# A second layernorm fed from centred summands instead of from the first one's finished output

## What is computed

```
t = t + _L0_ffn_ref(_ln_t(t), ...)         # layer 0's experts; their output is out
#   _L0_ffn_ref ends with
#   out = _layer_norm(out + x, gamma, beta)  # (v - mean) * rsqrt(var + 1e-5) * gamma + beta, over channels
x = _from_tokens(t, x)
x = x + _L1_conv_ref(_ln_c(x), ...)        # layer 1's mixer; _ln_c: (v - mean) / sqrt(var + 1e-6), over channels
#   _L1_conv_ref begins with 1x1, 3x3 and 5x5 convolutions of its input, summed
```

## Time and profile before

| what | value |
|---|---|
| median of 3 runs | 191.16 us (191.05 to 191.4) |
| the profiled execution's own time | 190.52 us |
| its span, first to last instruction | 188.7 us |
| granted TensorE clock, mean | 1.0 of full speed |
| busy: TensorE / its weight loads | 176.2 us (93%) / 87.0 us (46%) |
| busy: VectorE / ScalarE / GpSimd | 116.7 (62%) / 123.9 (66%) / 44.8 us (24%) |

### The profile page before, as it was taken

One profiled execution on the slowest core, in us unless ns is written; L12 is line 12 of the kernel. 1 busy time (PEld: TensorE's weight loads), 2 busy tenths in 40 slices (PEclk: granted clock), 3 DMA queues, 4 the chain that ended last, 5 costly groups with the idle time before them and its releaser, 6 DMA issues.

```text
span 188.7 us, 3175 instructions
## 1 busy us (share of the span) xinstructions
PE 176.2 (93%) x1185; PEld 87.0 (46%) x1191; DVE 116.7 (62%) x312; ACT 123.9 (66%) x201; POOL 44.8 (24%) x62
## 2 busy tenths in 40 slices
PE   7999999999997999999999999999999996999991
PEld 2554324449786574322222355452224895353230
DVE  1476889758732744946545353586575798587565
ACT  2465997745438776765765650587775897588772
POOL 6162412000100102005973000020760022030660
PEclk9999999999999999999999999999999999999999
DMA  6999700000000000000000000000000000000001
GB/s 204 401 423 414 280 2 0 0 0 3 5 0 0 3 0 3 0 0 0 0 3 2 0 0 0 0 0 3 0 2 0 3 2 2 3 0 0 0 0 56
DMA packets 3088, 8.56 MB, mean 45 GB/s; under 512 B 521, under 2 KB 1041, under 8 KB 2945
## 3 DMA queue, kind: packets, MB, share of 16 engines
q1 hardware_dynamic: 2736, 7.73, 10.3%
q0 software_dynamic: 192, 0.50, 0.7%
q10 hardware_dynamic: 144, 0.13, 0.3%
HBM read 8.10 MB, written 0.26 MB: 44 GB/s over the span
## 4 chain that ended last, share of the span: by engine, by line
PE 67%; DVE 13%; ACT 8%; POOL 6%; issue 4%; POOLq 1%; ACTq 0%; DVEq 0%
PE bank L454 13%; PE banks L386 7%; PE banks L312 7%; PE banks L387 6%; POOL total L1620 6%; PE bank L325 5%; PE banks L650 4%; PE bank L317 4%; PE banks L369 3%; ACT hidden L893 2%; ACT rstd L861 2%; PE bank L434 1%; PE banks L625 1%; PE bank L397 1%; ACT sq_sim L979 1%
## 5 line engine op out<-in xcount | busy, mean ns | idle before, releaser
L893 ACT ACTIVATE hidden<-banks,pack_l 128x1024 f32<-128x1024 f32 x40 | 44.5, 1112 | 17.3 <-PE banks L387 16.6
L454 PE MATMUL bank<-hidden,w 128*64 128x512 f32 (+1 forms) x144 | 37.1, 593 | 0.7 <-ACT hidden L893 0.7
L386 PE MATMUL banks<-split_x,w_hi 128*128 128x512 f16 x64 | 24.6, 384 | 0.0
L387 PE MATMUL banks<-split_x,w_lo 128*128 128x512 f16 x64 | 24.3, 379 | 0.0
L312 PE MATMUL banks<-idle_work 128*128 128x512 bf16 x66 | 18.4, 408 | 1.5 <-DVE idle_work L1199 1.2
L1620 POOL TENSOR_TENSOR total<-total,term 128x512 f32<-128x512 f32 x12 | 17.1, 1422 | 1.9 <-DVE term L1176 1.3
L1597 POOL CAST split_x<-normed 64x256 f16<-64x256 f32 x12 | 6.1, 505 | 45.8 <-DVE normed L1081 42.1
L386 PEld LDWEIGHTS banks<-split_x,w_hi 128*128 128x128 f16 x64 | 6.2, 97 | 22.4 <-issue 13.4
L857 ACT ACTIVATE squares<-bank 128x256 f32<-128x256 f32 x18 | 6.9, 383 | 14.3 <-PE bank L317 12.8
L454 PEld LDWEIGHTS bank<-hidden,w 128*64 128x64 f32 x144 | 7.2, 134 | 14.1 <-issue 12.5
L1176 DVE TENSOR_TENSOR term<-relu_sim,bank 128x512 f32<-128x512 f32 x12 | 7.8, 684 | 7.8 <-PE bank L397 5.3
(11 more groups left out here) (320 smaller groups left out, 325.3 us busy)
## 6 DMA issues: line engine op xcount, KB each, us to landing
w_stage<-in_w SPq DMA_DIRECT2D x3, 512.0 KB, 12.7
w_stage<-in_w SPq DMA_DIRECT2D x1, 1024.0 KB, 9.2
conv<-in_conv SPq DMA_DIRECT2D x1, 800.0 KB, 7.3
w<-in_w SPq DMA_DIRECT2D x3, 256.0 KB, 12.9
w<-in_w SPq DMA_DIRECT2D x1, 512.0 KB, 9.9
toeplitz<-in_toeplitz SPq DMA_DIRECT2D x1, 512.0 KB, 10.5
gauss<-in_gauss SPq DMA_DIRECT2D x1, 512.0 KB, 12.0
pack_l<-in_pack_l SPq DMA_DIRECT2D x1, 469.0 KB, 11.3
```

The costliest lines, as they stand in the source:

```text
L386: mm(out, w1_hi[l][:, at:at + 128], split_x[h][:, :], start=True, stop=False)
L387: last = mm(out, w1_lo[l][:, at:at + 128], split_x[h][:, :], start=False, stop=True)
L454: last = mm(out[64 * h:64 * h + 64, cut], w2[l][:, (f * NE + e) * CH:(f * NE + e + 1) * CH], hidden[v % 3][:, h * 512 + cut.start:h * 512 ...
L893: act(hidden[u % 3][:, :], both[u % 2][:, :], ACT.Gelu, bias=P(f"l{l}", "e_b1")[:, e * fc + f:e * fc + f + 1]).then_inc(S["moe_gelu"], 1)
```

## The change

C is the centring matrix. Centring x2 gives C·x2 = C·diag(gamma)·C·total times the root, plus C·(x1 + beta), since the root is one number per pixel. The kernel now makes the 128x128 matrix C·diag(gamma)·C on the chip, at its start (VectorE: `gamma_rows`; TensorE: one product into `bank[3]`; ScalarE: a copy into `both_centred`). At the seam TensorE makes `both_centred` times `total` (`centred_scaled`) and C times `x1_beta` (`centred_input`), the latter for chunk 0 ahead of the last expert's `down`. VectorE multiplies the first by norm 2's root and adds the second; the sum is norm 3's centred input, in SBUF. ScalarE squares it from there. Norm 3's root goes into `rnorm`, so that norm 2's stays in `rstd`. x2 itself is made later on VectorE, behind the rounding rests. The filler after layer 0's experts is gone, and those in front of norm 3's averages are one each.

```diff
-        LAYER_TAIL = [1, 5, 6, 0]
+        LAYER_TAIL = [0, 5, 6, 0]
...
+        centred_x1 = (bank[1][:, 0:PIX], bank[3][:, PIX:2 * PIX])
...
+            def centred_input(j):
+
+                pe.wait_ge(S["x1_beta"], 1)
+                mm(centred_x1[j], P("first", "center"), chunk(x1_beta, j), start=True, stop=True)
+
+            def centred_scaled(j):
+
+                mm(bank[2 + j][:, 0:PIX], both_centred[:, :], chunk(total, j), start=True, stop=True)\
+                    .then_inc(S["x2_terms"], 1)
...
+                if l == 0:
+                    centred_input(0)
                 down(units - 1)
...
+            pe.wait_ge(S["gamma_centre"], 1)
+            mm(bank[3][:, 0:128], P("first", "center"), gamma_rows[:, :], start=True, stop=True).then_inc(S["gamma_centre"], 1)
+            busy(NORM_TAIL[0], bank[0][:, :])
             for j in range(INNER):
                 pe.wait_ge(S["l0_xn"], j + 1)
+                if j:
+                    pe.wait_ge(S["gamma_centre"], 3)
...
-            norm(2, total, lambda j: pe.wait_ge(S["l0_term"], 2 * L0_KEPT + j + 1))
-
-
-
-            for j in range(INNER):
-                center(3, j, x[2], x_ready(2))
-                busy(2, bank[0][:, :])
-                average(3, j)
+            for j in range(INNER):
+                center(2, j, total, lambda j: pe.wait_ge(S["l0_term"], 2 * L0_KEPT + j + 1))
+            for j in range(INNER):
+                average(2, j)
+            centred_scaled(0)
+            centred_input(1)
+            centred_scaled(1)
+            busy(1, bank[0][:, :])
+            average(3, 0)
+            busy(1, bank[0][:, :])
+            average(3, 1)
             busy(NORM_TAIL[3], bank[0][:, :])
...
-                act(chunk(squares, j), bank[4 + j][:, 0:PIX], ACT.Square).then_inc(S["ln_squared"], 1)
+                act(chunk(squares, j), chunk(normed[3], j) if k == 3 else bank[4 + j][:, 0:PIX], ACT.Square)\
+                    .then_inc(S["ln_squared"], 1)
...
+            sc.wait_ge(S["gamma_centre"], 2)
+            act(both_centred[:, :], bank[3][:, 0:128], ACT.Copy).then_inc(S["gamma_centre"], 1)
...
+            ve.wait_ge(S["first_loaded"], 16)
+            ve.wait_ge(S["l0_loaded"], 16)
+            TS(gamma_rows[:, :], P("first", "center"), P("l0", "gamma"), None, ALU.mult).then_inc(S["gamma_centre"], 1)
...
-            ve.wait_ge(st.sem, x1b)
-            for j in range(INNER):
-                norm_chunk(2, j)
+            for j in range(INNER):
+                ve.wait_ge(S["ln_rstd"], 2 * 2 + j + 1)
+                ve.wait_ge(S["x2_terms"], j + 1)
+                TT(chunk(term[1], j), bank[2 + j][:, 0:PIX], chunk(rstd, j), ALU.mult).then_inc(S["ln_out"], 1)
                 ve.wait_ge(S["ln_out"], 2 * 2 + j + 1)
-                STT(chunk(x[2], j), chunk(normed[2], j), P("l0", "gamma"), chunk(x1_beta, j), ALU.mult, ALU.add)\
-                    .then_inc(S["x_ready"], 1)
-
-
-            for j in range(INNER):
-                norm_chunk(3, j)
+                TT(chunk(normed[3], j), centred_x1[j], chunk(term[1], j), ALU.add).then_inc(S["ln_centered"], 1)
+
+            for j in range(INNER):
+                ve.wait_ge(S["ln_rstd"], 2 * 3 + j + 1)
+                ve.wait_ge(S["ln_squared"], 2 * 3 + j + 1)
+                TT(chunk(normed[3], j), chunk(normed[3], j), chunk(rnorm, j), ALU.mult).then_inc(S["ln_out"], 1)
                 for h in range(HALVES):
                     ve.wait_ge(S["v_hi"], 2 * j + h + 1)
                     here, other = slice(64 * h, 64 * h + 64), slice(64 - 64 * h, 128 - 64 * h)
                     TT(chunk(padded[h], j)[other, :], chunk(normed[3], j)[here, :], chunk(padded[h], j)[here, :],
                        ALU.subtract).then_inc(S["v_lo"], 1)
+            ve.wait_ge(S["x1_beta"], 1)
+            for j in range(INNER):
+                st.link(TT(chunk(normed[2], j), bank[4 + j][:, 0:PIX], chunk(rstd, j), ALU.mult))
+                STT(chunk(x[2], j), chunk(normed[2], j), P("l0", "gamma"), chunk(x1_beta, j), ALU.mult, ALU.add)\
+                    .then_inc(S["x_ready"], 1)
```

More of the change, by code:

```diff
@@ L127, in metaformer @@
             w1_split0 w1_split1 w1_split2 w1_split3 w2_loaded0 w2_loaded1 w2_loaded2 w2_loaded3 x_loaded
-            x_ready y_ps z_ps z_rows""".split()
+            gamma_centre x1_beta x2_terms x_ready y_ps z_ps z_rows""".split()
         S = {n: sem(n) for n in names}
@@ L217, in metaformer @@
         context = sb("context", [128, 128])
+        gamma_rows = sb("gamma_rows", [128, 128])
+        both_centred = sb("both_centred", [128, 128])
         mix = sb("mix", [128, 128])
@@ L501, in _ @@
             pe.wait_ge(S["first_loaded"], 16)
-            norm(0, x[0], lambda j: pe.wait_ge(S["x_loaded"], 16))
+            for j in range(INNER):
+                center(0, j, x[0], lambda j: pe.wait_ge(S["x_loaded"], 16))
+            for j in range(INNER):
+                average(0, j)
+            pe.wait_ge(S["gamma_centre"], 1)
+            mm(bank[3][:, 0:128], P("first", "center"), gamma_rows[:, :], start=True, stop=True).then_inc(S["gamma_centre"], 1)
+            busy(NORM_TAIL[0], bank[0][:, :])
             for j in range(INNER):
                 pe.wait_ge(S["l0_xn"], j + 1)
+                if j:
+                    pe.wait_ge(S["gamma_centre"], 3)
                 for h in range(HALVES):
@@ L856, in square @@
                 sc.wait_ge(S["ln_centered"], 2 * k + j + 1)
-                act(chunk(squares, j), bank[4 + j][:, 0:PIX], ACT.Square).then_inc(S["ln_squared"], 1)
+                act(chunk(squares, j), chunk(normed[3], j) if k == 3 else bank[4 + j][:, 0:PIX], ACT.Square)\
+                    .then_inc(S["ln_squared"], 1)
             def inverse_deviation(k, j):
                 sc.wait_ge(S["ln_variance"], 2 * k + j + 1)
-                act(chunk(rstd, j), variance_ps(k, j), ACT.Abs_reciprocal_sqrt,
+                act(chunk(rnorm if k == 3 else rstd, j), variance_ps(k, j), ACT.Abs_reciprocal_sqrt,
                     bias=P("first", "eps6" if LN_EPS[k] == 1e-6 else "eps5")).then_inc(S["ln_rstd"], 1)
@@ L1305, in _ @@
             weight = lambda e, j: l0_weight[:, j * 8 + e:j * 8 + e + 1]
-            x1b = st.mark(TS(x1_beta[:, :], x[1][:, :], P("l0", "beta"), None, ALU.add))
+            TS(x1_beta[:, :], x[1][:, :], P("l0", "beta"), None, ALU.add).then_inc(S["x1_beta"], 1)
             for e in range(L0_KEPT):
```

## The result

The changed kernel takes 191.85 us (median of 18 runs) against 191.13 us of the kernel before in as many runs beside it: ratio 1.0037, 95% interval 1.0022 to 1.0053. It is slower by 0.7 us, with an interval of 0.4 to 1.0. The forecast was 191.5 us, range 191.0 to 192.0. The time lies in the range, but the case I thought likeliest was "no change", and the excess over the kernel before is twice the 0.33 us that I had worked out.

The account below looks back on a forecast made before the run. It took the engine-to-engine relay, VectorE's nearly gapless queue (0.13 us slack) and TensorE's channel-gate wait as bounds. Front minus 0.50, queue plus 1.73, less slack and overlap, gave plus 0.33: 191.5 us, range 191.0 to 192.0.

Parts of the forecast that it names:

- no change: Whole kernel: time within about 0.2% (0.38 us) of the kernel before; chance 0.45.
- Edits that I cost at nothing: x1's centring before the last down, 0 to plus 0.1 us; start's matrix product, 0 to plus 0.22; filler removal, nothing or minus 0.1.
- The front: Layernorm relay from layer 0's last expert to the first convolution tap: convolution starts 0.50 us earlier, at 42.48.
- Point 1: At the seam, the both_centred product stands behind two averages, ends at 37.89; VectorE's root product starts 37.92, 0.28 us late.
- Points 2 to 4: Relay after the root product: ScalarE's square starts 0.53 us earlier, SBUF reading adds 0.03, the rest keeps its shapes.
- the prediction's own sign: Front is wrong if the first tap does not move by half a microsecond.
- The queue: x2's four VectorE instructions before the weights' split take 1.73 us; channel gate's second product comes 0.33 us later, at 51.13.
- Sum: Front minus 0.50, queue plus 1.73, slack and earlier convolution used up, overlap regained minus 0.16: net plus 0.33 us.
- Absorbed: Rival: TensorE's stop at the channel gate costs nothing later, the 0.50 us stay won, 190.7 us; chance 0.12.
- Products not late: Rival: at the seam the root ends last, front gains 0.78, total plus 0.05, 191.2 us; chance 0.10.
- Clock: Rival: TensorE's clock falls in the new gap at 49.4, up to 4 us more, 195 us; chance 0.04.
- GpSimd's squaring over the scaling: Rival: before the channel gate, delayed squaring holds VectorE's mean scaling to 50.4, plus 0.25 us, 191.7 us; chance 0.14.

Follow-up runs that it names:

- Experiments 2: Changed kernel with the centring of x1's first chunk moved from ahead of the last expert's down product to behind the first both_centred product; ratio to the kernel before 1.0013.
- experiment 4: Changed kernel with x1's first chunk centred in the same place by two products of 64 output columns each; ratio to the kernel before 1.0014.
- experiment 7: Kernel before plus one centring product of x1's first chunk ahead of the last expert's down product, result unused; ratio 1.0012.
- experiment 8: Changed kernel with x2 in VectorE's gaps, x1's centring later, one start filler less, and first both_centred product between the averages; ratio to the kernel before 0.9985.
- experiment 1: Changed kernel with x2's four instructions moved from ahead of the weights' split into VectorE's gaps; ratio to the kernel before 1.0004.
- experiment 6: Kernel before plus four VectorE instructions of x2's shapes between the rounding rests and neg_scale, each waiting for the last, result unused; ratio 1.0048.
- experiment 9: Changed kernel with x2 in gaps, one start filler less, x1's centring as 64-column halves before the last down, both_centred product between averages; 189.86 us, ratio to before 0.9945.
- experiments 5: Changed kernel with x2 in VectorE's gaps, x1's centring behind the first both_centred product, and four start fillers instead of five; ratio to the kernel before 0.9971.

## Why the prediction was right and where it was wrong

**The step that failed is the paragraph "Edits that I cost at nothing"**, in two of its terms. For x1's centring I put 0 to 0.1 us, because 0.25 us of idle time and 0.27 of overlap made room for a product of 0.43. Experiments 2, 4 and 7 show 0.31 (0.30 in experiment 7): the overlap of load and tail, which I added to the room, is just what is lost when a 128-column product stands between 64-column ones. I had seen that overlap between products of one shape only, and took it for a property of all. The Trainium skill, "TensorEngine Tiling (Array Packing)", section "Key Properties", says that a change of the tiling mode drains the engine. The traces fit that, with 0.31 us for one product there and back and with 64-column passes that run in pairs; the page has no figure. The kernel declares no tiling mode, so that the drain is the mechanism is argued from the two idle stretches of the loads and not shown. For the start I put 0 and had plus 0.22 as a bound; it was plus 0.16: the cover was there for a quarter of the product only.

**The front.** Point 1 had the right wait and nearly its size. The product by the root is 1.67 us behind the averages' start; I had 1.59. TensorE's product ends as worked out (38.34 + 0.59 = 38.93, 1.56 behind 37.37), but VectorE starts 0.11 later and not 0.03. The step in between is a semaphore instruction of VectorE's own: an instruction carries one wait here, and of two waits the other stands ahead of it as an instruction by itself. In the trace that for TensorE's product (line 1360) comes at 38.98, and the product by the root 0.06 behind it. In experiment 8 the sum has the same step (38.98, then 39.05). The kernel before has it too, in its chain of waits between the root's end (37.54) and VectorE's 37.64, and I had not counted it:

```profile
37.57 0.02 DVEq L1080
```

The chain of waits of the changed kernel names another releaser (start us, length us, what):

```profile
38.11 0.92 ACT rstd L889 x2
...
39.04 0.44 DVE term L1361
```

It names ScalarE's roots, because the second chunk's ends at 39.03 by coincidence. The code waits for the first one's, and in experiment 8 VectorE's product starts at 38.19, when the second root (38.55) is not yet begun. Points 2 to 4, from there to the first tap, were 4.56 us forecast and measured. So the front gained 10.34 - 10.23 = 0.11 us from the last but one `down` to the first tap, where 0.50 was forecast: 0.31 went in the slot and 0.08 in the late start. By the prediction's own sign, a first tap that moves by half a microsecond, the front was wrong.

**The queue.** 1.73 us forecast, 1.72 measured. The first product of the gate follows the maximum by 0.56 us (0.60 forecast), the second the first by 0.70 (0.71). One small gain was missing in the sum: the maximum starts 0.08 us before the recorded end of the low part of the weights, where I let 0.03 pass. Behind the gate nothing had slack, as said. Of the 1.72 us only 0.67 come through (experiment 1): 0.19 go at the maximum, 0.69 at the gate's first product, to which TensorE comes 1.25 us behind the maximum when it has not to wait (49.12 and 50.37 in experiment 1) and now 0.56, and 0.17 between the gate's two products, mostly in the shorter `ca_in`.

**Sum.** Forecast plus 0.33. To that come 0.31 (slot), 0.08 (late product) and 0.16 (start), and off it about 0.11 for the maximum and 0.05 for the rest up to the gate: 0.72, where the distances give 0.70. The forecast's distance to the edge of "no change" was 0.05 us, so a mis-sized term of 0.3 was enough to turn the case. That the time still lies in the range is partly luck: the slot went 0.21 us past its bound, and 0.16 us of gains that the sum did not have made up for most of it.

**The rivals.** *Absorbed*: falls by experiments 1 and 6. *Products not late*: falls, they are late by 0.36; with them in time (experiment 9) the front gives 0.85. *Clock*: all forty slices stay at nine. In experiments 5 and 8 the last slice falls to seven, but the clock's record falls there at 186.0 and 186.6 us, behind TensorE's last product (184.0 and 184.2), and the time from the exponentials to the end is as before (133.6). *GpSimd's squaring over the scaling*: half of it happens. In experiment 6 the squaring starts at 51.22 under the low part of the weights and takes 0.96 us in place of 0.61; counted back from its end it ran from 51.57, 0.06 ahead of the maximum that follows VectorE's instruction. In the changed kernel it is 0.71 long for the same reason (51.37 - 0.61 = 50.76, again 0.06 ahead of the maximum). The Trainium skill, "SBUF — State Buffer", section "SBUF: two separate sides", says that such a pair block each other for a whole instruction; both rows agree. But the scaling, with one tensor input of one element per partition, ran in full beside the squaring, 0.14 us at 51.95 (51.15 in the changed kernel), so the 0.25 us of this rival did not come. And `ca_in` was 0.15 long, as forecast.

Not shown: the start's 0.16 in timed runs, where it is smaller than the intervals, and what sets the moment at which the clock's record begins.

## What to carry to other kernels

A gap between TensorE's products takes in another one at the price of its passes only if it has its neighbours' weight width (0.01 against 0.31 us here): read from the record what two neighbours of different shape cost, and not only how long the gap is. When an intermediate result leaves the relay and is still needed later, it has to go into measured idle time; put in front of a chain it costs its length less all the slack behind it, which has to be read at every engine that the chain passes (here 1.72 us became 0.67). A product that is taken off a path helps only if every input of the next instruction is early as well: move one and read which is last now.

## What the runs showed of the hardware that was not expected

- One product of full width between 64-column ones costs 0.30 us more than the same work in two halves, whose passes run in pairs (slot 1.65 and 1.35 us, changed kernel and experiment 4; 1.64 in experiment 7).
- The first eleven products of a program take 3.90 to 4.88 us from one execution to the next, with the same instructions, because their spacing halves (0.43 to 0.22 us) at a moment that lies anywhere from 3.95 to 7.02 us, where the trace's record of the clock begins. A comparison of two single spans of this kernel is uncertain by at least that much.
- On VectorE a chain in which each instruction waits for the one ahead cost 0.98 us for a pair, where a pair with one such wait cost 0.86 (experiment 6).
- A scaling of one element per partition with one tensor input (0.14 us) runs unhindered beside a GpSimd squaring that a long instruction of VectorE had held up (experiment 6), while `ca_in`, of one element and two tensor inputs, takes 0.31 us beside that squaring and 0.15 without it.
- Where VectorE's last wait is not the one that its instruction carries, 0.10 to 0.11 us pass from the recorded end of what it waits for to its start, against some 0.04 otherwise: in the changed kernel the product by the root starts at 39.04 behind TensorE's 38.93, in experiment 9, where the root is last, at 37.43 behind 37.39.
